# Norm statistics moved from ScalarE and GpSimd to VectorE, with every engine's order written anew

## The chip, the cores and the metric

The kernel runs on one core of one Trainium2 chip. The metric is device time in microseconds (us) of one execution. Its engines are TensorE (PE; its weight loads are the row PEld), VectorE (DVE), ScalarE (ACT), GpSimd (POOL) and SyncE (SP), which here only issues DMAs.

## The reference

Two transformer blocks in a row over 64 sequences of 64 rows by 256 features. What is computed, for each sequence:

```
x   = hidden
x  += attention(layernorm(x) @ w_qkv)        @ w_ao      # self, 16 heads of 16
x  += attention(layernorm(x) @ w_q, ctx @ w_kv) @ w_co   # cross, keys and values from ctx
x  += gelu(layernorm(x) @ w1) @ w2                       # mlp0
lat = x
y   = attention(lat @ q_w, concat(ctx, lat) @ kv_w) @ out_w + lat
out = gelu(rmsnorm(y) @ mlp_w1) @ mlp_w2 + lat           # mlp1
```

Each layernorm subtracts a row's mean and multiplies by one over the root of its variance plus an epsilon; the rmsnorm before the second MLP multiplies by one over the root of the mean square plus an epsilon. All biases, scales and masks are applied. Inputs and output are float32.

## The kernel before, in words

Two sequences make a unit of 128 rows, so there are 32 units, each a chain of the same stages: self attention, cross attention, mlp0, the attention over context and latents ("ctx" and "lat"), mlp1. Products run in float16 in two halves: each operand is written as a high part and a low part, and three matmuls stand for one (`w_hi` with high and low, `w_lo` with high). An activation gets its halves on the row-major side in `pair_*`, and one transposing DMA, issued by SP, brings both to the feature-major side in `turned_*` (or `heads_turned_*` for what attention gives). So a norm runs thus: VectorE adds a projection to the residual (`add_residual`, L1282, or `add_mlp`, L1298); the statistics; ACT applies them (`normalize`, L1920, `xn_*`); GpSimd rounds to the high half (`high_pair`, L2465); VectorE takes the low half (`low_pair`, L1174 and L1177); SP issues the transposing DMA (`across`, L2779); PE uses what it brings.

The statistics before the change are spread over three engines. For the three layernorms (self, cross, mlp0) VectorE runs `bn_stats` (L1165) and `bn_aggr` (L1168), and GpSimd in `root` runs three instructions on 128x1: variance plus epsilon (`var_*`, L2454), the power of minus one half (`rstd_*`, L2456), minus mean times that (`shift_*`, L2459). For the rmsnorm of mlp1 ACT squares and sums the row (`squared_rows`, L1928), and GpSimd runs L2454 and L2456.

No scheduler acts when the kernel is built. For each engine the order of the stages is written out by hand as a list of calls such as `moments(t - 3, "cross")`: a part that fills the pipeline, a loop `for t in range(FILL, SLOTS)` of 24 passes in which every stage of some unit stands once, and a part that drains it. The number taken from `t` is the lag of that stage; the last argument of PE's calls is the PSUM bank. Engines run their lists in order and wait on semaphores, so an instruction that waits holds up all behind it on its engine. SP issues all DMAs from one list too.

VectorE's other work in a pass: `k_spread` and `q_bias_self` (PSUM to SBUF), `masked`, `largest_score`, `shifted` (softmax on 128x512), `denominators` and `divided` (`over_*`, `heads_*`), `heads_low` (L1186), `hidden_lo` (L1288). GpSimd's: `plus_bias`, `added` (mask addend, L2507), `mask_add`, `mask_keys`, `ctx_high`, `ctx_low`, `shifted_ctx` (L2513).

## Time and profile before

| | |
|---|---|
| median of 3 runs | 1072.71 us (1070.87 to 1075.0) |
| profiled execution, its own time | 1074.24 us |
| its span in the trace | 1072.0 us |
| PE busy | 1002.5 us, 94% |
| VectorE busy | 949.5 us, 89% |
| ACT busy | 859.3 us, 80% |
| GpSimd busy | 671.7 us, 63% |
| mean granted TensorE clock | 0.978 |

Busy shares are averages over three stretches: the filling of the pipeline up to about 206 us, the loop up to about 937 us, and the drain. Within the loop every pass takes the same time and shows the same picture, so it is read per pass; the two ends have other limits. A span begins and ends with the first and last record of the trace; the execution's own time is 2.24 us longer.

### The profile page before, as it was taken

To read this page: it belongs to the slowest core of one execution; us is meant where nothing else is said; L and a number is where in the kernel's file an instruction comes from. 1 tells how busy PE (TensorE), PEld (TensorE's weight loads), DVE (VectorE), ACT (ScalarE), POOL (GpSimd) and SP (SyncE) were. 2 spreads that over 40 slices of the span, in tenths; PEclk is the share of its full clock that TensorE was granted. 3 is DMA by queue.
4 is the path that set the end of the run, shared out by engine and by line. 5 is a ranking of instruction groups with operands and counts; after the bars stand their busy time and mean duration, and the time that the engine had idled before them with its cause. 6 is when DMAs were issued, how large, how long until landed. Compare 5 with 4: busy or idle time off the path is not lost.

```text
span 1072.0 us, 46440 instructions
## 1 busy us (share of the span) xinstructions
PE 1002.5 (94%) x19180; PEld 892.1 (83%) x19180; DVE 949.5 (89%) x2008; ACT 859.3 (80%) x1967; POOL 671.7 (63%) x1037
## 2 busy tenths in 40 slices
PE   5777989999999999999999999999999999998988
PEld 5666878888888888888888888888888888887877
DVE  4887988999999999999999999999999999987763
ACT  3447689888888888888889888888888888787995
POOL 3787577666667666666666666666666666755320
PEclk9787999999999999999999999999999999999999
DMA  8652221223322222232222222222222222321111
GB/s 297 208 161 78 46 47 37 50 55 59 49 49 47 54 51 52 55 60 54 50 48 53 54 45 58 56 59 49 50 46 55 50 54 44 67 47 37 32 22 41
DMA packets 169699, 67.70 MB, mean 63 GB/s; under 512 B 151184, under 2 KB 167312, under 8 KB 168464
## 3 DMA queue, kind: packets, MB, share of 16 engines
q1 hardware_dynamic: 169488, 64.72, 26.8%
q8 instruction: 152, 2.49, 1.0%
q14 instruction: 59, 0.48, 0.2%
HBM read 26.93 MB, written 4.19 MB: 29 GB/s over the span
## 4 chain that ended last, share of the span: by engine, by line
PE 30%; ACT 23%; DVE 18%; issue 11%; DMA 11%; SPq 5%; POOL 2%; ACTq 0%; POOLq 0%; DVEq 0%
PE psum L457 9%; ACT staging L2007 7%; PE psum L598 7%; ACT hid_mlp L2007 6%; PE psum L630 5%; DMA turned_cross<-pair_cross 4%; PE psum L470 4%; DMA heads_turned_cross<-heads_pair_cross 3%; ACT L1993 3%; DVE mx_lat L1239 3%; PE psum L564 2%; SPq L2779 2%; ACT parts_mlp L2016 2%; ACT probT_self L1993 1%; SPq L2761 1%
## 5 line engine op out<-in xcount | busy, mean ns | idle before, releaser
L2513 POOL TENSOR_TENSOR late<-late,mx_ctx 128x512 f32<-128x512 f32 x64 | 67.7, 1057 | 103.9 <-DVE mx_ctx L1245 103.9
L2507 POOL TENSOR_TENSOR prob_cross<-prob_cross,add_cross 128x512 f32<-128x512 f32 x64 | 91.1, 1441 | 57.5 <-DVE prob_cross L1229 57.4
L2507 POOL TENSOR_TENSOR prob_self<-prob_self,add_self 128x512 f32<-128x512 f32 x64 | 81.9, 1282 | 38.5 <-DVE prob_self L1229 32.3
L2007 ACT ACTIVATE hid_mlp<-psum,folded,undo_in 128x128 f32<-128x128 f32 x256 | 96.2, 458 | 7.8 <-PE psum L457 7.1
L2007 ACT ACTIVATE staging<-psum,cols,undo_in 128x128 f32<-128x128 f32 x256 | 97.8, 484 | 2.8 <-PE psum L457 2.3
L630 PE MATMUL psum<-hi_m,parts_mlp 128*128 128x256 f16 x512 | 95.3, 275 | 0.3 <-DVE parts_mlp L1288 0.3
L630 PE MATMUL psum<-hi_n,staging 128*128 128x256 f16 x512 | 93.9, 273 | 1.4 <-DVE staging L1288 1.4
L457 PE MATMUL psum<-turned_mlp,hi_m 128*128 128x128 f16 x1024 | 92.3, 219 | 3.1 <-DMA turned_mlp<-pair_mlp 1.4
L457 PE MATMUL psum<-turned_mlp,hi_n 128*128 128x128 f16 x1024 | 90.4, 220 | 0.8 <-DMA turned_mlp<-pair_mlp 0.3
L2484 POOL TENSOR_TENSOR xb<-x,rows 128x256 f32<-128x256 f32 x96 | 82.8, 873 | 10.2 <-DVE x L1298 5.7
L457 PE MATMUL psum<-turned_mlp,lo_m 128*128 128x128 f16 x512 | 88.7, 219 | 0.0
L457 PE MATMUL psum<-turned_mlp,lo_n 128*128 128x128 f16 x512 | 88.1, 220 | 0.0
L457 PEld LDWEIGHTS psum<-turned_mlp,hi_m 128*128 128x128 f16 x1024 | 78.3, 98 | 9.4 <-issue 5.5
L1993 ACT ACTIVATE late<-psum 128x512 f32<-128x512 f32 x128 | 71.7, 596 | 12.3 <-PE psum L584 12.2
L457 PEld LDWEIGHTS psum<-turned_mlp,hi_n 128*128 128x128 f16 x1024 | 78.9, 98 | 2.3 <-issue 1.1
L630 PE MATMUL psum<-lo_m,parts_mlp 128*128 128x256 f16 x256 | 70.2, 274 | 0.0
L630 PE MATMUL psum<-lo_n,staging 128*128 128x256 f16 x256 | 69.8, 273 | 0.0
L598 PE MATMUL psum<-val_ctx,late 128*64 128x34 f32 x1024 | 63.7, 228 | 0.7 <-issue 0.5
L598 PE MATMUL psum<-val_lat,late 128*64 128x34 f32 x1024 | 63.0, 226 | 0.0
L1288 DVE SCALAR_TENSOR_TENSOR parts_mlp<-hid_mlp,hidden_up,parts_mlp 128x512 f16<-128x512 f32 x64 | 57.0, 891 | 6.1 <-ACT parts_mlp L2016 5.1
L598 PEld LDWEIGHTS psum<-val_ctx,late 128*64 128x64 f32 x1024 | 53.3, 140 | 6.3 <-issue 5.8
L1985 ACT ACTIVATE val_lat<-psum,undo 64x128 f32<-64x128 f32 x128 | 47.3, 369 | 12.8 <-PE psum L470 11.0
(262 smaller groups left out, 3766.4 us busy)
## 6 DMA issues: line engine op xcount, KB each, us to landing
xin<-in_x SPq DMA_DIRECT2D x32, 128.0 KB, 2.1
late<-in_ctxT SPq DMA_DIRECT2D x4, 1024.0 KB, 6.0
ctxT<-in_ctxT SPq DMA_DIRECT2D x32, 128.0 KB
late<-in_x SPq DMA_DIRECT2D x4, 1024.0 KB, 5.1
out<-xb SPq DMA_DIRECT2D x32, 128.0 KB, 2.0
staging<-in_w_m SPq DMA_DIRECT2D x2, 1024.0 KB, 7.1
staging<-in_w_n SPq DMA_DIRECT2D x2, 1024.0 KB, 5.0
mask<-in_mask_cross SPq DMA_DIRECT2D x32, 32.0 KB
```

The lines of the kernel that those rows point to most:

```text
L457: last = e.matmul(out_ap, wt[name][:, k, c:c + P], xs[:, k, :], start=(n == 0), stop=(n == 3 * KH - 1))
L470: last = e.matmul(ps[:, 0:H], xs[:, k, :], wt[name][:, k, c:c + H], start=(n == 0), stop=(n == 3 * KH - 1))
L598: last = e.matmul(ps[S * a:S * a + S, p * VW:(p + 1) * VW], probT[s][a][:, j, :], val[s][:, a, p, :], start=(n == 0), stop=(n == len(sets) ...
L630: last = e.matmul(ps[:, 0:H], a, wt, start=(g == 0 and n == 0), stop=(g == 1 and n == 11))
L1239: e.tensor_reduce(max_of(t, h).rearrange("p (r n) -> p r n", r=2), src, AX.X, ALU.max).then_inc(sem["max_" + t], 1)
L1288: e.scalar_tensor_tensor(part[t][g][:, 512:1024], hid[t][g][:, :], hidden_up[t], part[t][g][:, 0:512], ALU.mult, ALU.subtract).then_inc(se ...
L1985: last = e.activation(o, i, ACT.Copy, scale=scale)
L1993: e.activation(probT[t][a][:, :, :], src, ACT.Exp).then_inc(sem["probT_" + t], 1)
L2007: last = e.activation(hid[t][g][:, j * P:(j + 1) * P], ps[:, j * P:(j + 1) * P], ACT.Gelu_apprx_tanh, bias=b1[:, 4 * g + j:4 * g + j + 1], ...
L2484: e.tensor_tensor(o[:, :], a[:, :], row, ALU.add).then_inc(sem["plus_bias_" + t], 1)
L2507: e.tensor_tensor(ch, ch, over_heads(a[:, :]), ALU.add).then_inc(sem["added_" + t], 1)
L2513: e.tensor_tensor(ch, ch, over_keys(max_of("ctx", h)), ALU.subtract).then_inc(sem["shifted_ctx"], 1)
```

## The change

Statistics. For all four norms VectorE now computes the moments and the variance plus epsilon. `moments` runs four instructions for each norm: `bn_stats`, `bn_aggr`, and then for a layernorm minus the mean (`minus_mean_*`) and the shrunk variance (`var_*`); for mlp1 the mean square from mean and variance, and the same with epsilon. ACT's `squared_rows` is gone. GpSimd's `root` keeps the power, and for a layernorm the product of minus mean and `rstd`. Core of the diff:

```diff
 # VectorE, moments(u, t)
-                src, steps, n = residual(t, u), sem["moments_" + t], 2 * u
-                q.wait_ge("moments_" + t, n)
+                src, shrink = residual(t, u), 2.0 ** (-2 * XHAT_UP)
+                steps, n = sem["moments_" + t], 4 * u
...
-                    q.wait_ge({"cross": "x_self", "mlp0": "x_cross"}[t], u + 1)
+                    q.wait_ge({"cross": "x_self", "mlp0": "x_cross", "mlp1": "x_lat"}[t], u + 1)
                 e.bn_stats(bn[t][:, :], src[:, :]).then_inc(steps, 1)
                 q.wait_ge("moments_" + t, n + 1)
-                q.wait_ge("rstd_" + t, 3 * u)
                 e.bn_aggr(mv[t][:, :], bn[t][:, :]).then_inc(steps, 1)
+                q.wait_ge("moments_" + t, n + 2)
+                if t == "mlp1":
+                    e.scalar_tensor_tensor(mean_square[:, :], mv[t][:, 0:1], mv[t][:, 0:1], mv[t][:, 1:2],
+                                           ALU.mult, ALU.add).then_inc(steps, 1)
+                    q.wait_ge("moments_" + t, n + 3)
+                    e.tensor_scalar(var[t][:, :], mean_square[:, :], L1_EPS, shrink, ALU.add, ALU.mult).then_inc(steps, 1)
+                else:
+                    q.wait_ge("rstd_" + t, 2 * u)
+                    e.tensor_scalar(minus_mean[t][:, :], mv[t][:, 0:1], -1.0, None, ALU.mult).then_inc(steps, 1)
+                    e.tensor_scalar(var[t][:, :], mv[t][:, 1:2], L0_EPS, shrink, ALU.add, ALU.mult).then_inc(steps, 1)
 # ScalarE
-            def squared_rows(u):
-                q.wait_ge("x_lat", u + 1)
-                q.wait_ge("rstd_mlp1", 2 * u)
-                e.activation(squared[:, :], residual("mlp1", u)[:, :], ACT.Square, scale=1 / ROOT_H,
-                             accum_out=mean_square[:, :]).then_inc(sem["mean_square_mlp1"], 1)
 # GpSimd, root(u, t)
-                e.tensor_scalar(var[t][:, :], src, eps, shrink, ALU.add, op1=ALU.mult).then_inc(done, 1)
-                q.wait_ge("rstd_" + t, n + 1)
-                e.tensor_tensor(rstd[t][:, :], var[t][:, :], minus_half[:, :], ALU.pow).then_inc(done, 1)
+                q.wait_ge("moments_" + t, 4 * u + 4)
+                q.wait_ge("x_lo_mlp1" if t == "mlp1" else "xn_" + t, u)
+                e.tensor_tensor(rstd[t][:, :], var[t][:, :], minus_half[:, :], ALU.pow).then_inc(sem["rstd_" + t], 1)
                 if t != "mlp1":
-                    q.wait_ge("rstd_" + t, n + 2)
-                    e.tensor_scalar(shift[t][:, :], mv[t][:, 0:1], rstd[t][:, 0:1], -1.0, ALU.mult, op1=ALU.mult).then_inc(done, 1)
+                    q.wait_ge("rstd_" + t, 2 * u + 1)
+                    e.tensor_tensor(shift[t][:, :], minus_mean[t][:, :], rstd[t][:, :], ALU.mult).then_inc(sem["rstd_" + t], 1)
 # SP's loop, a line or two of the new lists
-                load_rest(t - 2)
                 across(t - 3, "cross")
                 across(t - 4, "mlp0")
+                across(t - 7, "mlp1")
+                load_rest(t - 1)
```

Orders. All five lists are new, in the fill, the loop and the drain, and so are PE's bank numbers. Some lags differ: PE's `qk_self` goes from `t - 1` to `t - 2` and stands first in the pass, `v_cross` from `t - 2` to `t - 3`; on VectorE the second half of the "lat" softmax and the low half of cross attention's heads go to the start of the next pass; `load_rest` is one unit earlier. On VectorE the second half of self attention's subtraction of the maximum and both halves of cross attention's (`shifted`) now stand in a row, after all four maxima. In GpSimd's list `plus_bias` of lat stands between `root` and `high_pair` of cross, and `plus_bias` of mlp0 between `root` and `high_pair` of mlp0; before, each pair was adjacent.

The first place is VectorE in the loop, where the layernorm of cross attention gets its statistics. Before:

```order
L1282 SCALAR_TENSOR_TENSOR x<-psum,undo,xb 128x256
L1165 BN_STATS bn_cross<-x 128x6
L1168 BN_AGGR mv_cross<-bn_cross 128x2
L1177 TENSOR_TENSOR pair_self<-xn_self,pair_self 128x256
L1165 BN_STATS bn_self<-xin 128x6
L1168 BN_AGGR mv_self<-bn_self 128x2
L1282 SCALAR_TENSOR_TENSOR x<-psum,undo,xb 128x256
L1165 BN_STATS bn_mlp<-x 128x6
L1168 BN_AGGR mv_mlp<-bn_mlp 128x2
```

The same place now, beginning with the statistics of mlp1 (`bn_mlp<-xb`):

```order
L1165 BN_STATS bn_mlp<-xb 128x6
L1167 BN_AGGR mv_mlp<-bn_mlp 128x2
L1170 SCALAR_TENSOR_TENSOR mean_square<-mv_mlp 128x1
L1173 TENSOR_SCALAR var_mlp<-mean_square 128x1
L1189 SCALAR_TENSOR_TENSOR q_self<-psum,down_q,folded 128x256
L1213 SCALAR_TENSOR_TENSOR spread_self<-psum,down_of_two_self,bias_of_two_self 128x2x128
L1297 SCALAR_TENSOR_TENSOR staging<-staging,hidden_up 128x512
L1291 SCALAR_TENSOR_TENSOR x<-psum,undo,xb 128x256
L1165 BN_STATS bn_cross<-x 128x6
L1167 BN_AGGR mv_cross<-bn_cross 128x2
L1176 TENSOR_SCALAR minus_mean_cross<-mv_cross 128x1
L1177 TENSOR_SCALAR var_cross<-mv_cross 128x1
```

What was two instructions for a layernorm is four in a row, and mlp1 has four that VectorE did not have.

The second place is VectorE further on in the pass, around the low half of the latents' attention heads (`heads_pair_lat`). Before it stands behind cross attention's softmax (`prob_cross`) and mlp0's low half (`parts_mlp`):

```order
L1239 TENSOR_REDUCE mx_cross<-prob_cross 128x8
L1204 SCALAR_TENSOR_TENSOR spread_lat<-psum,down_of_two_lat,bias_of_two_lat 128x2x128
L1258 TENSOR_TENSOR prob_cross<-prob_cross,mx_cross 128x512
L1288 SCALAR_TENSOR_TENSOR parts_mlp<-hid_mlp,hidden_up,parts_mlp 128x512
L1186 TENSOR_TENSOR heads_pair_lat<-heads_lat,heads_pair_lat 128x256
L1239 TENSOR_REDUCE mx_ctx<-late 128x8
```

Now it stands ahead of the masking of cross attention's scores (`prob_cross<-psum,mask`):

```order
L1267 TENSOR_TENSOR prob_self<-prob_self,mx_self 128x512
L1213 SCALAR_TENSOR_TENSOR spread_lat<-psum,down_of_two_lat,bias_of_two_lat 128x2x128
L1195 TENSOR_TENSOR heads_pair_lat<-heads_lat,heads_pair_lat 128x256
L1186 TENSOR_TENSOR pair_self<-xn_self,pair_self 128x256
L1238 TENSOR_TENSOR prob_cross<-psum,mask 128x512
L1248 TENSOR_REDUCE mx_self<-prob_self 128x8
```

GpSimd's addition to `prob_cross` waits for that masking, so it comes after both low halves now.

The third place is SP's queue around the transposing DMA of cross attention's input (`turned_cross`). Before, the four loads of `load_rest` stand right in front of it:

```order
L2779 DMA_TRANSPOSE turned_self<-pair_self 128x4x128
L2758 DMA ctxT<-in_ctxT 128x256
L2759 DMA mask<-in_mask_cross 128x64
L2761 DMA keys_i<-in_mask_keys 64x64 x2
L2779 DMA_TRANSPOSE turned_cross<-pair_cross 128x4x128
```

Now they come after it and after those of mlp0 and mlp1:

```order
L2780 DMA_TRANSPOSE heads_turned_cross<-heads_pair_cross 128x4x128
L2738 DMA xin<-in_x 128x256
L2771 DMA_TRANSPOSE turned_cross<-pair_cross 128x4x128
L2771 DMA_TRANSPOSE turned_mlp<-pair_mlp 128x4x128 x2
L2750 DMA ctxT<-in_ctxT 128x256
```

Only the load of `xin` is left between the two transposing DMAs there.

## Rows read from the trace of the kernel before

**Rows 1.** The page's first part: busy us, share of the span, instructions.
```profile
PE 1002.5 (94%) x19180; PEld 892.1 (83%) x19180; DVE 949.5 (89%) x2008; ACT 859.3 (80%) x1967; POOL 671.7 (63%) x1037
```

**Rows 2.** Fill, loop, drain: length; PE, PEld, DVE, ACT, POOL busy; PEclk, DMA share, GB/s.
```profile
0.00:206.20 206.20, 170.41 (x2838) 148.75 (x2839) 165.27 (x378) 133.89 (x289) 133.67 (x238) 0.90 0.43 119
206.20:936.60 730.40, 710.54 (x14166) 637.46 (x14163) 692.24 (x1442) 615.76 (x1436) 486.26 (x724) 1.00 0.25 52
936.60:1072.00 135.40, 121.56 (x2184) 105.89 (x2181) 92.02 (x190) 109.66 (x244) 51.76 (x77) 0.97 0.18 35
```

**Rows 3.** Waits from 400 to 704.4 us: who waited for whom; total, times, longest.
```profile
DVE over_self L1264 <- PE psum L598: 3.6, 10, 0.4
PE psum L598 <- ACT probT_self L1993: 3.0, 10, 0.3
PE psum L457 <- DMA turned_cross<-pair_cross: 2.5, 4, 0.9
DVE x L1282 <- PE psum L470: 2.2, 4, 0.7
PE psum L470 <- DMA heads_turned_cross<-heads_pair_cross: 1.9, 4, 0.7
DVE parts_mlp L1288 <- ACT parts_mlp L2016: 1.8, 6, 0.3
DVE prob_cross L1229 <- PE psum L564: 1.4, 4, 0.8
DVE x L1298 <- PE psum L630: 1.1, 5, 0.2
```

**Rows 4.** VectorE's timeline in one pass of the loop, start and duration in us.
```profile
709.51 0.42 DVE L1165 BATCH_NORM_STATS2 bn_self<-xin 128x6 f32<-128x256 f32 x1
709.96 0.18 DVE L1168 BATCH_NORM_AGGREGATE mv_self<-bn_self 128x2 f32<-128x6 f32 x1
710.06 0.47 DVE L1282 SCALAR_TENSOR_TENSOR x<-psum,undo,xb 128x256 f32<-128x256 f32 x1
```

**Rows 5.** VectorE's timeline in the setup: small instructions, the second needing the first.
```profile
12.28 0.16 DVE L1045 TENSOR_SCALAR power<-psum 128x2 int32<-128x2 int32 x1
12.48 0.33 DVE L1099 TENSOR_SCALAR row_up_qkv<-cols,power 128x1 f32<-128x1 f32 x2
```

**Rows 6.** Groups by line on VectorE from 400 to 704.4 us: busy, mean ns | idle before.
```profile
L1288 DVE SCALAR_TENSOR_TENSOR parts_mlp<-hid_mlp,hidden_up,parts_mlp 128x512 f16<-128x512 f32 x20 | 18.3, 913 | 2.2 <-ACT parts_mlp L2016 1.8
L1258 DVE TENSOR_TENSOR prob_self<-prob_self,mx_self 128x512 f32<-128x512 f32 x20 | 17.6, 879 | 0.3
L1258 DVE TENSOR_TENSOR prob_cross<-prob_cross,mx_cross 128x512 f32<-128x512 f32 x20 | 17.3, 864 | 0.3
L1288 DVE SCALAR_TENSOR_TENSOR staging<-staging,hidden_up 128x512 f16<-128x512 f32 x20 | 14.8, 741 | 0.0
L1258 DVE TENSOR_TENSOR late<-psum,mx_ctx 128x512 f32<-128x512 f32 x21 | 14.3, 679 | 0.0
L1186 DVE TENSOR_TENSOR heads_pair_lat<-heads_lat,heads_pair_lat 128x256 f16<-128x256 f32 x10 | 9.5, 948 | 0.0
L1174 DVE SCALAR_TENSOR_TENSOR pair_mlp<-xb,rstd_mlp,pair_mlp 128x256 f16<-128x256 f32 x10 | 7.9, 790 | 0.0
L1191 DVE SCALAR_TENSOR_TENSOR pair_lat<-x,power,pair_lat 128x256 f16<-128x256 f32 x10 | 4.8, 484 | 0.0
L1186 DVE TENSOR_TENSOR heads_pair_self<-heads_self,heads_pair_self 128x256 f16<-128x256 f32 x10 | 4.2, 415 | 0.0
```

**Rows 7.** One piece of the chain of waits in the drain: start, us, what.
```profile
1008.91 0.52 ACT squared L1928 x2
```

**Rows 8.** Timeline around the transposing DMA of cross attention's input.
```profile
712.26 1.12 SPq L2761 DMA_DIRECT2D keys_i<-in_mask_keys  x2
712.41 0.42 DVE L1177 TENSOR_TENSOR pair_cross<-xn_cross,pair_cross 128x256 f16<-128x256 f32 x1
713.50 1.21 SPq L2779 DMA_TRANSPOSE turned_cross<-pair_cross  x1
```

More of the change, by code:

```diff
@@ new lines, in _ @@
+            add_mlp(0, "mlp0")
+            largest_score(2, "cross", 1)
+            shifted(2, "cross", 0)
+            add_residual(3, "self")
+            low_pair(1, "mlp0")
+            lat_low(0)
+            k_spread(5, "self", 1)
+            shifted(2, "cross", 1)
+            denominators(4, "self")
+            divided(4, "self")
+            moments(3, "cross")
+            masked(5, "self", 0)
+            heads_low(4, "self")
+            powers(0, "n2")
+            masked(5, "self", 1)
@@ L1573, in _ @@
                 moments(t - 3, "cross")
[L1574 to L1575 removed]
+                k_spread(t - 2, "self", 1)
                 add_residual(t - 4, "cross")
@@ new lines, in _ @@
+            heads_low(UNITS - 4, "cross")
+            k_spread(UNITS - 3, "cross", 0)
+            hidden_lo(UNITS - 8, "mlp1", 0)
+            largest_both(UNITS - 6, 1)
+            add_residual(UNITS - 7, "lat")
+            shifted(UNITS - 6, "lat", 1)
+            k_spread(UNITS - 3, "cross", 1)
+            moments(UNITS - 7, "mlp1")
+            add_residual(UNITS - 3, "self")
+            moments(UNITS - 3, "cross")
+            add_residual(UNITS - 4, "cross")
+            moments(UNITS - 4, "mlp0")
@@ L2637, in _ @@
-            shifted_ctx(2, 1)
+            ctx_high(4)
+            ctx_low(4)
+            shifted_ctx(1, 0)
+            shifted_ctx(1, 1)
+            mask_keys(3)
+            mask_add(4)
+            root(3, "mlp0")
+            high_pair(3, "mlp0")
+            high_pair(6, "self")
+            plus_bias(3, "mlp0")
+            root(0, "mlp1")
+            added(4, "cross", 0)
+            added(4, "cross", 1)
+            low_mlp(0, "n2")
+            plus_bias(5, "self")
+            plus_bias(1, "lat")
```

1834 lines of the change are left out of this document (891 added, 943 removed).

## The prediction, written before the changed kernel ran

> **What bounds the kernel now.** I read the page's busy shares first. PE leads with 94%, VectorE follows with 89%, ACT has 80%, GpSimd 63% [rows 1]. An average over a filling and draining pipeline says little, so I next cut the span into fill, loop and drain [rows 2]. In the loop the picture is tighter: of 730.4 us PE is busy 710.5 (97.3%), VectorE 692.2 (94.8%), ACT 615.8 (84.3%), GpSimd 486.3 (66.6%), with the TensorE clock fully granted. In the stretch from 400 to 704.4 us a line that a pass runs twice on VectorE stands 20 times [rows 6], so ten passes take 304.4 us: 30.44 us a pass, and the loop's 24 passes fill the middle stretch. Per pass PE works 29.6 us and VectorE 28.84. The loop is thus held by two engines at once: PE has 0.8 us to spare, VectorE 1.6 us. Fill and drain together have less pressure on VectorE (165 of 206 us, 92 of 135 us), and in the drain ACT is busier than VectorE (110 of 135 us).
>
> Third, the waits of ten passes [rows 3]. PE waits for transposing DMAs (2.5 and 1.9 us in ten passes, 0.44 us a pass) and for the exponentials of self attention (0.30 us a pass). VectorE's waits for other engines are five pairs that add up to 10.1 us, 1.01 us a pass. The rest of its 1.60 us of idle time, 0.59 us, is its own: short gaps in which one of its instructions waits for the one before it. These gaps stay whatever PE does. So what VectorE needs for a pass is 30.44 - 1.01 = 29.43 us. The reader is to see that an addition of more than 1.01 us to VectorE's pass makes it the engine that sets the pass.
>
> **What the statistics cost VectorE.** Prices are taken from start to start, since neighbours overlap by some 0.08 us. `bn_stats` to the dependent `bn_aggr` is 709.96 - 709.51 = 0.45 us; `bn_aggr` to an independent successor is 710.06 - 709.96 = 0.10 us [rows 4]. A small instruction to one that needs it is 12.48 - 12.28 = 0.20 us. Two independent ones on 128x1 take 0.33 us together, so the second adds 0.13 us to the first's 0.20 [rows 5]. No row shows a successor waiting on `bn_aggr`; its 0.18 us and the gap of 0.03 us that stands between `bn_stats` (end 709.93) and `bn_aggr` make 0.21.
>
> - mlp1, new on VectorE: 0.45 + 0.21 + 0.20 + 0.13 = 0.99 us.
> - Each layernorm: the wait behind `bn_aggr` goes from 0.10 to 0.21, and two small instructions come at 0.13: + 0.37 us, for three norms 1.11 us.
> - Sum: 2.10 us a pass. From below: if each added small instruction cost no more than its 0.13 us slot and the waits hid, 0.45 + 0.10 + 8 x 0.13 = 1.6 us. From above: if each of the eight cost its dependent 0.20 us, 0.45 + 0.21 + 1.6 + 0.33 (three times 0.11) = 2.6 us. I take 2.10, built from the nearest rows.
>
> With all else equal VectorE needs 29.43 + 2.10 = 31.53 us a pass, 1.09 us more than a pass takes now.
>
> **What else changes on VectorE: its collisions with GpSimd.** Some lines with both inputs in SBUF are longer than their twins [rows 6]: `parts_mlp` 913 against 741 ns, `prob_self` 879 and `prob_cross` 864 against 679 for the same operation out of PSUM, `heads_pair_lat` 948 against 415, `pair_mlp` of mlp1 790 against 484. Per pass: 0.34 + 0.40 + 0.37 + 0.53 + 0.31 = 1.95 us. A new order deals these anew. `heads_pair_lat` now stands before the masking of cross attention's scores, for which GpSimd's big addition waits, so GpSimd has little to do then: - 0.5. The first half of self attention's subtraction likewise: - 0.2. Against that, three of the four halves of `shifted` for self and cross now come in a row, just when GpSimd has `keys_mask` and the context's halves to do; I count + 0.3. Net - 0.4 us, so 31.1 us a pass. The bounds are no collisions at all (31.53 - 1.95 = 29.6, and then PE decides) and half as many again (32.5). I stay near the present value, since no row says how a new order falls.
>
> The Trainium skill ("SBUF — State Buffer", Who interferes with whom) says that a VectorE instruction with two SBUF inputs contends with a GpSimd instruction that reads SBUF, and that the loser fully blocks. The trace agrees with the first part, as the twins above show. By that rule `bn_stats`, with one input, is safe.
>
> **What the others gain.** ACT loses `squared_rows`, 0.52 us a unit [rows 7]. In the loop ACT has 4.8 us a pass to spare, so it is worth nothing there. In the drain ACT is the busiest, and seven or so units pass through its norm there: at most - 3.6 us; I take - 2, as other waits lie between. GpSimd loses four small instructions a pass and is at 67%: nothing in the loop. The chain of one norm is no shorter: VectorE does in 0.2 to 0.3 us what GpSimd did.
>
> **What the new orders gain PE.** Before, `pair_cross` is ready at 712.83 and its DMA is issued at 713.50, because SP is still issuing the loads of `load_rest` until 713.38 [rows 8]. Those loads now come later, so the DMA goes out some 0.6 us sooner, and PE has more products between the projection and `q_cross`. That removes most of the 0.44 us a pass that PE waits for DMAs. Alone it would make the pass 30.0 us. But when VectorE needs 31.1 this only turns into other waiting of PE: worth nothing. Its cover is VectorE's length; if that falls away, the 0.44 us count. Bank numbers cost nothing while PE waits anyway.
>
> **Sum.** Loop: 24 x (31.1 - 30.44) = + 15.8 us. Fill: VectorE has 41 us of idle time there, so the 2.1 us of each of its units mostly fit in; I take + 1. Drain: - 2. Together + 15 us. The profiled execution is 1074.24 us, 2.24 beside its span of 1072.0, so it would be 1089; the median of the runs shown is 1.5 us below it, 1072.7, and by that the new median is 1087.7. Forecast: 1088 us.
>
> **Rivals.**
>
> A, faster: PE stays the bound. If the new order has so few collisions that VectorE needs under 30.0 us (1.5 of the 1.95 us gone), the transposing DMAs' 0.44 us come through: 24 x -0.44 = - 10.6, with the drain - 2: 1060 us. For it: an order that spreads the work may do this, and the list of VectorE puts several colliding lines where GpSimd waits. Against it: GpSimd is busy two thirds of the time, and VectorE would have to be busy over 98% of a pass. It decides from a need of 30.4 downward. Chance 0.22.
>
> B, no change: collisions fall by about 1 us, the need is 30.4 and the pass stays: 1070 to 1076, say 1073. Chance 0.15.
>
> C, much slower: VectorE stalls in its own list. In GpSimd's new list `plus_bias` of lat and of mlp0 stand between the roots and the casts of cross and mlp0, and `low_pair` follows closely on VectorE, with all its later work behind it. A GpSimd instruction takes 486.3 / 724 = 0.67 us in the mean [rows 2]; if the casts of both come later by that and half of it reaches VectorE, it stalls 0.7 us and needs 31.8 us a pass: 24 x 1.36 = 33, with the ends 32, 1105 us. It decides from the point at which a cast ends after VectorE's list has come to the low half. Against it: the addition may pass while ACT applies the norm. Chance 0.11.
>
> The same section of the Trainium skill says that a `tensor_scalar` can enter a two-port mode and then contend with GpSimd too. As a mechanism here: seven of the new small instructions would each wait for a GpSimd instruction under way; with GpSimd busy two thirds of the time and half of the mean 0.67 us still to go, 0.22 us each, 1.6 us a pass, 24 x 1.6 = 38 us on top of the forecast, 1126 us. The setup's small instructions show none of it [rows 5]. Chance 0.02.
>
> The forecast itself (31.1, from 30.6 to 31.6) has 0.50.
>
> **How the numbers follow.** A difference of 0.5%, 5.4 us, is about what a measurement of this kernel can tell from none. Slower by more than that: the forecast but for its lower edge (0.48), C (0.11) and the two-port mechanism (0.02): 0.61. Within: B but for its lower edge (0.13) and the edge of the forecast (0.02): 0.15. Faster: A (0.22) and B's edge (0.02): 0.24. The range leaves out about half of A below, a third of C and the two-port mechanism above: 1062 to 1108; the forecast's own is 1076 to 1100.
>
> **What the profile after would show.** If right: in the loop VectorE is busy over 97% and its waits for PE and ACT are nearly gone, while PE's share falls to about 95.5% and PE waits for VectorE (its `k_spread`, `hidden_lo`, `shifted`) rather than for DMAs; VectorE's busy sum is near 1000 us; the small instructions of `moments` stand 0.13 and 0.20 us apart; `heads_pair_lat` falls to about 0.45 us. Wrong if VectorE stays under 96% busy with a pass of 30.4 us or less (A or B), or if a pass is over 31.6 us; if the change stands in fill or drain, my split is wrong even with the right total.

## The result, and the profile after

The changed kernel takes 1077.34 us (median of 17 runs, 1074.03 to 1079.99), the kernel before 1072.71 us in the same comparison (17 runs, 1069.88 to 1078.22): a ratio of 1.0034, 95% interval 1.0018 to 1.0050. It is slower, as forecast, but by 0.3%, not by the forecast 1.4%. The profiled execution took 1074.87 us, its span is 1073.0 us.

The page's first part and the clock row of its second answer to [rows 1]. The digits of PEclk are tenths of the granted clock in 40 equal slices.

```profile
PE 995.5 (93%) x19180; PEld 887.4 (83%) x19180; DVE 976.1 (91%) x2328; ACT 845.7 (79%) x1903; POOL 629.5 (59%) x909
...
PEclk9898999999999999999999999999999999999999
```

VectorE's busy sum rose by 26.6 us, where "near 1000" had been said. The kernel before has `PEclk9787999` at the head of the same row. The next two windows are the changed kernel's fill and loop, and answer to [rows 2] (length; PE, PEld, DVE, ACT, POOL busy; clock, DMA share, GB/s).

```profile
0.00:200.92 200.92, 163.00 (x2832) 142.72 (x2833) 169.68 (x424) 132.62 (x283) 127.08 (x218) 0.95 0.44 122
200.92:906.33 705.41, 682.37 (x13573) 613.69 (x13571) 676.57 (x1611) 582.60 (x1336) 431.98 (x599) 1.00 0.28 52
```

In the loop PE is busy 96.7% and VectorE 95.9%. Neither is full, though the prediction wanted VectorE over 97%.

A finer cut comes from VectorE's timeline: the starts of its last operation of a unit (`xb<-psum,undo_out,x` of `add_mlp` for mlp1), 32 in each kernel. Before, the first stands at 202.78, the 24th at 902.28 and the last at 1069.40 us. After, they stand at 196.58, 902.35 and 1070.33. So the fill is 6.2 us shorter, 23 passes are 6.3 us longer (a pass 30.69 for 30.41 us in the mean; the median of the 23 is 30.56 for 30.35), and the drain is 0.9 us longer. These two profiled executions differ in span by 1.0 us, the medians by 4.6: the profiled one of after (below, "after" is the changed kernel) is at the quick end of its 17 runs.

Waits from 400 to 704.4 us, VectorE's (the two largest) and PE's, answer to [rows 3]: who waited for whom, total us, times, longest.

```profile
DVE parts_mlp L1297 <- ACT parts_mlp L2026: 5.5, 10, 0.7
DVE pair_mlp L1186 <- POOL pair_mlp L2457: 1.4, 7, 0.2
...
PE psum L584 <- DVE prob_cross L1267: 5.5, 10, 0.8
PE psum L564 <- DVE spread_ctx L1213: 3.0, 10, 0.3
PE psum L470 <- DMA heads_turned_cross<-heads_pair_cross: 0.3, 1, 0.3
```

PE no longer waits for DMAs (0.03 us a pass, 0.44 before) but for VectorE (0.85 us a pass), as forecast. Yet VectorE itself still waits, ten times in ten passes, for ACT's `parts_mlp`. That is the sign of the miss: if VectorE's sum set the pass, it would wait for nobody.

The statistics in VectorE's timeline (start, duration) answer to [rows 4].

```profile
612.95 0.41 DVE L1165 BATCH_NORM_STATS2 bn_mlp<-xb 128x6 f32<-128x256 f32 x1
613.39 0.18 DVE L1167 BATCH_NORM_AGGREGATE mv_mlp<-bn_mlp 128x2 f32<-128x6 f32 x1
613.61 0.22 DVE L1170 SCALAR_TENSOR_TENSOR mean_square<-mv_mlp 128x1 f32<-128x1 f32 x1
613.87 0.15 DVE L1173 TENSOR_SCALAR var_mlp<-mean_square 128x1 f32<-128x1 f32 x1
613.94 0.47 DVE L1189 SCALAR_TENSOR_TENSOR q_self<-psum,down_q,folded 128x256 f32<-128x256 f32 x1
...
615.94 0.43 DVE L1165 BATCH_NORM_STATS2 bn_cross<-x 128x6 f32<-128x256 f32 x1
616.40 0.18 DVE L1167 BATCH_NORM_AGGREGATE mv_cross<-bn_cross 128x2 f32<-128x6 f32 x1
616.62 0.16 DVE L1176 TENSOR_SCALAR minus_mean_cross<-mv_cross 128x1 f32<-128x1 f32 x1
616.69 0.14 DVE L1177 TENSOR_SCALAR var_cross<-mv_cross 128x1 f32<-128x1 f32 x1
616.75 0.48 DVE L1213 SCALAR_TENSOR_TENSOR spread_self<-psum,down_of_two_self,bias_of_two_self 128x256 f32<-128x256 f32 x1
```

mlp1 costs 613.94 - 612.95 = 0.99 us, to the hundredth what was forecast, but partly by luck: a small instruction that needs the one before it starts 0.26 us after it (613.61 to 613.87), not 0.20, and the instruction behind the last follows after 0.07 us, not 0.13, and the two errors cancel. A layernorm costs 616.75 - 615.94 = 0.81, against 0.55 before: + 0.26, forecast + 0.37. Two independent small instructions start 0.07 us apart, not 0.13. The sum is 0.99 + 3 x 0.26 = 1.8 us a pass, for 2.10.

The colliding lines answer to [rows 6] (busy, mean ns | idle before).

```profile
L1267 DVE TENSOR_TENSOR prob_cross<-prob_cross,mx_cross 128x512 f32<-128x512 f32 x20 | 20.3, 1052 | 0.0
L1267 DVE TENSOR_TENSOR prob_self<-prob_self,mx_self 128x512 f32<-128x512 f32 x20 | 15.8, 790 | 0.3
L1297 DVE SCALAR_TENSOR_TENSOR parts_mlp<-hid_mlp,hidden_up,parts_mlp 128x512 f16<-128x512 f32 x20 | 15.5, 775 | 5.5 <-ACT parts_mlp L2026 5.5
L1186 DVE TENSOR_TENSOR pair_mlp<-xn_mlp,pair_mlp 128x256 f16<-128x256 f32 x10 | 5.8, 583 | 1.7 <-POOL pair_mlp L2457 1.4
L1183 DVE SCALAR_TENSOR_TENSOR pair_mlp<-xb,rstd_mlp,pair_mlp 128x256 f16<-128x256 f32 x10 | 4.7, 470 | 0.0
L1195 DVE TENSOR_TENSOR heads_pair_lat<-heads_lat,heads_pair_lat 128x256 f16<-128x256 f32 x10 | 4.1, 413 | 0.0
```

`heads_pair_lat` fell from 948 to 413 ns, `pair_mlp` of mlp1 from 790 to 470, `parts_mlp` and `prob_self` by 138 and 89 twice a pass; `prob_cross` rose from 864 to 1052, twice a pass, and is now the worst. Over all 23 passes, durations beyond those of the undisturbed twins fall from about 2.1 to about 1.2 us a pass: - 0.94, forecast - 0.4. Taking a pass less VectorE's waits for other engines (30.41 - 1.10 = 29.3 before, 30.69 - 0.78 = 29.9 after; "need" below), VectorE needs 29.9 us. The forecast was 31.1. The two measured prices would make 29.3 + 1.8 - 0.94 = 30.2, so some 0.3 us of the fall is not placed.

So what sets 30.56 us? The chain of waits from 600 to 632 us (start, us, what; the last piece is the first, one pass later):

```profile
600.38 0.73 ACT parts_mlp L2026
...
601.13 0.75 DVE parts_mlp L1297
...
603.22 1.96 DVE prob_cross L1267 x2
...
607.15 0.79 DVE spread_ctx L1213 x2
...
608.08 0.70 PE psum L564 x32
...
624.42 0.68 PE psum L457 x12
...
625.96 1.28 ACT L2017
...
629.42 1.50 ACT hid_mlp L2017 x4
...
630.93 0.73 ACT parts_mlp L2026
```

A ring, that is a chain of waits which comes back to its own first piece one pass later: ACT's hidden layer, seven microseconds of VectorE, 17 us of PE without a gap, ACT with a table load (L2017, 1.28 us), and back, 30.55 us later. The chain goes this way in all 23 passes. From the start of one engine's piece to the start of the next one's, the medians are 6.95 us for VectorE, 17.04 for PE and 6.56 for ACT, 30.55 together. VectorE's statistics of mlp1 and of the norms (612.95 to 618.5) lie beside PE's part of the ring. `prob_cross` lies in it, with its collision: 2 x 0.37 us.

### The profile page after: what moved, and what is told of

The parts are those of the page before. It is cut to its first block, busy times and chain, and to the rows that moved or that the text cites. A ratio compares the mean times of both kernels' runs of the same rounds, so it can differ in the third digit from the quotient of the medians.

```text
span 1073.0 us, 46470 instructions
## 1 busy us (share of the span) xinstructions
PE 995.5 (93%) x19180; PEld 887.4 (83%) x19180; DVE 976.1 (91%) x2328; ACT 845.7 (79%) x1903; POOL 629.5 (59%) x909
## 4 chain that ended last, share of the span: by engine, by line
PE 43%; DVE 26%; ACT 19%; issue 9%; POOL 1%; DMA 1%; SPq 1%; ACTq 0%; POOLq 0%; DVEq 0%
PE psum L470 11%; PE psum L457 9%; PE psum L598 7%; PE psum L630 7%; ACT hid_mlp L2017 7%; DVE prob_cross L1267 5%; PE psum L564 5%; ACT L2017 3%; DVE mx_ctx L1248 3%; PE psum L584 3%; DVE parts_mlp L1297 2%; ACT parts_mlp L2026 2%; DVE spread_ctx L1213 2%; DVE mx_cross L1248 2%; ACT staging L2017 1%
## 5 line engine op out<-in xcount | busy, mean ns | idle before, releaser
L2499 POOL TENSOR_TENSOR prob_self<-prob_self,add_self 128x512 f32<-128x512 f32 x64 | 86.9, 1374 | 67.2 <-DVE prob_self L1238 64.3
L2017 ACT ACTIVATE hid_mlp<-psum,folded,undo_in 128x128 f32<-128x128 f32 x256 | 95.5, 455 | 3.5 <-PE psum L457 3.0
L2017 ACT ACTIVATE staging<-psum,cols,undo_in 128x128 f32<-128x128 f32 x256 | 92.9, 460 | 2.7 <-PE psum L457 2.0
L630 PE MATMUL psum<-hi_m,parts_mlp 128*128 128x256 f16 x512 | 90.0, 273 | 0.8 <-DVE parts_mlp L1297 0.8
L2476 POOL TENSOR_TENSOR xb<-x,rows 128x256 f32<-128x256 f32 x96 | 72.2, 752 | 8.5 <-DVE x L1307 4.6
L2003 ACT ACTIVATE late<-psum 128x512 f32<-128x512 f32 x128 | 66.7, 602 | 6.4 <-PE psum L584 5.7
L1297 DVE SCALAR_TENSOR_TENSOR parts_mlp<-hid_mlp,hidden_up,parts_mlp 128x512 f16<-128x512 f32 x64 | 50.1, 783 | 17.1 <-ACT parts_mlp L2026 16.9
L2448 POOL TENSOR_TENSOR rstd_mlp<-var_mlp,minus_half 128x1 f32<-128x1 f32 x64 | 35.4, 553 | 47.1 <-DVE var_mlp L1173 44.7
L1267 DVE TENSOR_TENSOR prob_cross<-prob_cross,mx_cross 128x512 f32<-128x512 f32 x64 | 62.5, 1010 | 0.0
```

The lines of the kernel that those rows point to most:

```text
L630: last = e.matmul(ps[:, 0:H], a, wt, start=(g == 0 and n == 0), stop=(g == 1 and n == 11))
L1267: e.tensor_tensor(in_tiles(prob[t][h][:, :]), src, top, ALU.subtract).then_inc(sem["shifted_" + t], 1)
L1297: e.scalar_tensor_tensor(part[t][g][:, 512:1024], hid[t][g][:, :], hidden_up[t], part[t][g][:, 0:512], ALU.mult, ALU.subtract).then_inc(se ...
L2003: e.activation(probT[t][a][:, :, :], src, ACT.Exp).then_inc(sem["probT_" + t], 1)
L2017: last = e.activation(hid[t][g][:, j * P:(j + 1) * P], ps[:, j * P:(j + 1) * P], ACT.Gelu_apprx_tanh, bias=b1[:, 4 * g + j:4 * g + j + 1], ...
L2476: e.tensor_tensor(o[:, :], a[:, :], row, ALU.add).then_inc(sem["plus_bias_" + t], 1)
```

## The experiments

Pass is the median of the 23 passes and, behind it, their mean; need as above. Pass and need come from one profiled execution each. Each kernel ran beside the kernel before on the same chip; ratios are to that kernel, with 95% intervals.

| | median us (runs) | ratio | pass | mean | need |
|---|---|---|---|---|---|
| before | 1072.4 to 1074.8 (17 to 25) | 1 | 30.35 | 30.41 | 29.3 |
| after | 1077.34 (17) | 1.0034 [1.0018, 1.0050] | 30.56 | 30.69 | 29.9 |
| e1 new orders, old statistics | 1105.99 (5) | 1.0300 [1.0274, 1.0326] | 31.39 | 31.38 | 28.9 |
| e2 old orders, new statistics | 1098.03 (4) | 1.0233 [1.0206, 1.0259] | 31.21 | 31.39 | 31.2 |
| e3 new orders, mlp1's square on ACT | 1090.67 (5) | 1.0160 [1.0133, 1.0186] | 30.84 | 30.92 | 29.3 |
| e4 GpSimd holds | 1070.02 (12) | 0.9977 [0.9961, 0.9993] | 30.38 | 30.40 | 29.5 |
| e5 as e1, square early | 1099.50 (5) | 1.0256 [1.0231, 1.0282] | 31.20 | 31.19 | 28.9 |
| e6 extra outside the ring | 1079.32 (9) | 1.0055 [1.0036, 1.0074] | 30.64 | 30.79 | 30.1 |
| e7 extra inside the ring | 1084.22 (6) | 1.0111 [1.0087, 1.0134] | 30.88 | 30.95 | 30.2 |
| e8 before, loads later | 1070.20 (12) | 0.9980 [0.9961, 0.9998] | 30.33 | 30.37 | 29.5 |
| e9 hold, old statistics | 1100.48 (5) | 1.0227 [1.0202, 1.0252] | 31.17 | 31.14 | 28.7 |
| e10 hold, addition later | 1075.24 (12) | 1.0008 [0.9992, 1.0024] | 30.60 | 30.61 | 29.8 |
| e11 layernorms' statistics old | 1099.46 (6) | 1.0226 [1.0188, 1.0263] | 31.42 | 31.41 | 29.6 |
| e12 small ones in the norms' chain | 1081.71 (9) | 1.0079 [1.0049, 1.0110] | 30.86 | 30.88 | 30.0 |
| e13 the same elsewhere | 1077.14 (12) | 1.0030 [1.0006, 1.0054] | 30.56 | 30.68 | 29.9 |
| e14 hold, heads later | 1081.35 (11) | 1.0076 [1.0051, 1.0102] | 30.87 | 30.91 | 29.9 |

Theory 1 is the prediction's, a sum: VectorE's work sets the pass. Theory 2, a cycle (the ring), came with the profile after.

**e1 and e2, the two halves of the change.** e1 keeps the new orders and banks and takes back the statistics (`moments`, `root` and `squared_rows` as before):

```
                  exponential(t - 6, "lat", 0)
+                 squared_rows(t - 7)
                  exponential(t - 6, "ctx", 0)
...
                  shifted(t - 6, "lat", 1)
-                 moments(t - 7, "mlp1")
```

> The changed kernel's orders, lags and banks with the statistics as before the change: no moments of mlp1 on VectorE, squared_rows back on ACT (five calls ahead of scaled_high in the loop), three small instructions in GpSimd's root, two instead of four in moments. Theory 1 (the statistics are what lengthens the pass; the new orders by themselves help): VectorE's list loses some 1.6 us a pass (0.99 for mlp1, 0.24 for each layernorm, less two small gaps that come back), PE becomes the bound, the pass falls from 30.68 to about 30.0 us, and with the 6 us that the new fill saves the time is about 1058 us, ratio to before 0.986. Theory 2 (the statistics hide in VectorE's idle time; the new order itself made the pass 0.27 us longer through the chain ACT parts_mlp, VectorE shifted, PE): 1074 to 1078 us, ratio 1.002 to 1.005.

e2 is the kernel before with the new `moments` and `root`, `moments(t - 7, "mlp1")` behind `add_residual(t - 7, "lat")` and no `squared_rows`.

> The orders, lags and banks of before with the statistics of the changed kernel: moments of mlp1 right behind add_residual of lat on VectorE, four instructions in each moments, squared_rows gone from ACT, root without the variance. Theory 1: VectorE needs 29.4 us a pass of before plus 1.6 to 1.7, some 31.0, since the collisions with GpSimd stay about 2 us a pass; 24 passes of 0.5 to 0.6 us more, 1085 us, ratio 1.012. Theory 2: the pass stays at 30.4 us, 1071 to 1075 us, ratio 1.000. If my blind sum of 2.1 us for the statistics was right, 1090 us.

In the old orders the sum holds as a mechanism: need and pass are both 31.2 us, and VectorE waits for next to nothing in ten passes. Its size was missed: theory 1 had said 1085 us, and it came to 1098. A part of that is a collision that the edit made worse: `parts_mlp` takes 1215 ns in the mean in e2 and took 913 before, 0.6 us a pass. With the statistics' 1.8 this would be + 2.4 us, and the need grew by 1.9, so 0.5 us is not placed here either.

```profile
DVE parts_mlp L1297 <- ACT parts_mlp L2026: 1.2, 4, 0.3
DVE prob_cross L1238 <- PE psum L564: 0.9, 1, 0.9
```

The prediction's line "with all else equal 31.53" is this kernel. e1 missed by far, and on its own edit: GpSimd waited 22.4 us in ten passes for the square, twice the 11.2 of the kernel before, since it stood late in ACT's list. It was no fair test of the statistics.

**e3 and e5, work taken off VectorE in the new orders.** e3 puts only mlp1's square back on ACT, placed as in e1; e5 is e1 with `squared_rows(t - 7)` at the head of ACT's loop.

> The changed kernel with only the statistics of mlp1 back on ACT (squared_rows) and GpSimd (variance plus epsilon); the layernorms keep their four instructions on VectorE. Theory 1: 0.99 of the 1.6 us leave VectorE, the pass is 30.0 to 30.2 us, 1060 to 1065 us, ratio 0.990. If PE's own length of 29.7 us and its waits set the pass from there, e1 is hardly faster than this one. Theory 2: no change against the changed kernel, ratio 1.003.

> The changed kernel with all of the old statistics, as in e1, but in the loop ACT's squared_rows stands at the head of its list, right after VectorE's lat addition, instead of in front of scaled_high's neighbours: so GpSimd's root of mlp1 should not wait for it as it did in e1. VectorE needs some 28.3 us a pass. Theory of a sum (VectorE's work sets the pass): the loop falls by 24 x 1.6 us, to 1040 to 1060 us. Theory of a cycle (ACT hidden layer -> VectorE mx_cross, prob_cross, spread -> PE -> ACT sets 30.5 to 30.9 us a pass, and the statistics stand outside it): 1070 to 1082 us, VectorE idle for over 2 us a pass, prob_cross still at about 1000 ns. If GpSimd's root of mlp1 is late again (ACT squared among its waits with over 0.5 us a pass), the test is again not fair.

Both are slower, though VectorE needs 0.6 and 1.0 us a pass less. By the mark set for e5, a wait for the square of over 0.5 us a pass, neither is a quite fair test: it is 2.4 us in e3 and 0.59 in e5. But VectorE stood idle 2.3 us a pass in e5 for others, which a sum cannot explain, and e11, e6 and e7 below, which have no square on ACT, say the same. So theory 1 is dead in the new orders.

e3 is explained by the ring. Its chain goes the changed kernel's way in all 23 passes, and the piece that grew is VectorE's, from 6.95 to 7.23 us, as the pair of `prob_cross` now takes 2.29 us for 1.96: GpSimd's work fell differently onto it. For e5's 31.20 the ring as told ("the statistics stand outside it") is not enough. e5 is slower at the ends too: from the start to the first unit's last operation e5 takes 205.4 us and after 196.6, and behind the 24th unit's 174.5 against 170.6. So of e5's 22 us some 12 lie in the loop.

With e2 the change is a square of four: old orders 1072.7 and (new statistics) 1098.0; new orders 1099.5 (old statistics) and 1077.3.

**e4, the collision in the ring.** GpSimd starts its context work only when VectorE is through with `prob_cross`:

```
+ def hold(u): q.wait_ge("shifted_cross", 2 * u + 2)
...
+                 hold(t - 3)
                  mask_keys(t - 3)
```

> The changed kernel with one more wait in GpSimd's loop: before mask_keys it waits until VectorE has done both halves of cross attention's shifted, so that keys_mask, the context's halves and plus_bias of self no longer run beside them. Theory 1 (collisions are part of VectorE's bound): prob_cross falls from 1010 to about 690 ns and the second half of prob_self from 0.84 to 0.69 us, VectorE's pass loses 0.8 to 0.9 us, and the pass goes to 30.0 us, 1062 us, ratio 0.990. GpSimd has 5.1 us of work behind the wait, and about 5.5 us until mx_ctx lets it go on, so the wait itself costs at most 0.3 us a pass. Rival: if not collisions but another limit (PE, the chain through ACT) sets the pass, prob_cross gets shorter and the time stays at ratio 1.003; if the hold delays shifted_ctx, it is slower, 1.006.

```profile
L1267 DVE TENSOR_TENSOR prob_cross<-prob_cross,mx_cross 128x512 f32<-128x512 f32 x20 | 12.9, 684 | 0.0
L1195 DVE TENSOR_TENSOR heads_pair_self<-heads_self,heads_pair_self 128x256 f16<-128x256 f32 x10 | 6.9, 688 | 0.0
```

`prob_cross` fell by 0.37 us twice a pass, the pass by only 0.18 (the mean by 0.29, and the time by 7.3 us): a second ring (ACT `staging`, table load, `probT_self`, VectorE's heads and `late`, PE, ACT), 30.33 us long, takes over in all 23 passes, and GpSimd's displaced work collides with `heads_pair_self` in it. It is the only version of the new orders quicker than the kernel before, by 0.23%.

**e6 and e7, one `bn_stats` outside and inside the ring.** The same 0.42 us instruction at one of two places, the first in e6, the second in e7:

```
+ def extra(u):
+     q.wait_ge("rows_ready", 1)
+     e.bn_stats(spare[:, :], rows[:, 0, :])
...
                  moments(t - 7, "mlp1")
+                 extra(t)
...
                  shifted(t - 3, "cross", 1)
+                 extra(t)
```

> The changed kernel with one more bn_stats of 128x256 a pass on VectorE (its result unused, its input a constant row), placed right behind the statistics of mlp1, outside the cycle. VectorE needs 29.9 + 0.34 to 0.41 = 30.3 us a pass, still below 30.69. Cycle: same time as the changed kernel, 1075 to 1079. Sum: 24 x 0.34 to 0.41 more, 1085 to 1087.

> The same additional bn_stats, now between the two halves of cross attention's shifted and the second half of spread_lat, which the cycle passes through (between parts_mlp and spread_ctx). Cycle: 24 x 0.34 to 0.41 = 8 to 10 us slower than the changed kernel and than e6, 1085 to 1087 (a little less if GpSimd's additions move off prob_cross). Sum: the same as e6, whichever that is.

The median pass grew by 0.08 us outside and by 0.32 inside (the mean by 0.11 and 0.27, the median time by 2.0 and 6.9 us), with a need of 30.1 and 30.2. e6's interval overlaps the changed kernel's, e7's does not. The chain says the same: in e7 the ring's VectorE piece grew from 6.95 to 7.27 us and the others stayed; in e6 the chain passes the additional instruction in none of 23 passes. This is the ring's signature: the place decides, not the engine's sum. Outside it isn't free to the last hundredth: PE's piece is 17.12 us for 17.04, and five of e6's passes are over 31.1 us where after has two. Its profiled execution is also the slowest of its nine.

**e8, the DMAs.** In the kernel before, SyncE's `load_rest(t - 2)` goes behind `across(t - 4, "mlp0")`.

> The kernel before with one edit: in the loop SyncE issues the loads of load_rest behind the transposes of cross and mlp0, not in front of them. The context is used some 15 us later than it lands, so nothing should miss it. If PE's waits for transposes (0.44 us a pass) are worth their size: 24 x 0.3 to 0.44 faster, 1062 to 1066. If they are only turned into other waiting of PE: 1070 to 1074, with the waits for DMAs gone and others, for VectorE or ACT, in their place.

PE's waits for DMAs did not go, they moved (the pair of [rows 3] for `turned_cross` still has 1.6 us in two waits):

```profile
PE psum L470 <- DMA heads_turned_cross<-heads_pair_cross: 2.8, 6, 0.8
PE psum L457 <- DMA turned_mlp<-pair_mlp: 1.9, 5, 0.5
```

The gain is 0.2%, at the edge of what the interval can tell from none, and the price of the 0.44 us stays open.

**e9, e11, e12, e13: what the new statistics give back.** e9 is e4 with e5's statistics; e11 is the changed kernel with only the layernorms' statistics as before; e12 and e13 add two `tensor_scalar` on 128x1, whose result nobody uses, to GpSimd, e13 at the first place and e12 at the second:

```
+ def small(u):
+     for i in range(2):
+         e.tensor_scalar(spare[i][:, :], minus_half[:, :], 1.0, 1.0, ALU.add, op1=ALU.mult)
...
+                 small(t)
                  root(t - 7, "mlp1")
...
+                 small(t)
                  root(t - 4, "mlp0")
```

> e5 (new orders, all of the old statistics, squared_rows early) with the hold of e4 on GpSimd: against e4 it differs in the statistics alone, with the collision on prob_cross gone in both. Sum: VectorE needs 1.6 us a pass less than in e4, so 24 x 1.6 faster than e4, or as far as PE lets it: 1040 to 1060. Cycle: the statistics stand outside, so nothing is won: 1066 to 1076, and up to 1090 if GpSimd's longer list (var, rstd, shift in a row) holds up spread_cross again. Either way e5's pass of 31.20 us should fall by the 0.6 us that its prob_cross lies over two undisturbed ones.

> The changed kernel with the statistics of the three layernorms as before (bn_stats and bn_aggr on VectorE, var, rstd and shift on GpSimd), those of mlp1 all on VectorE as in the change. If the layernorms' chain on GpSimd is what makes the new orders need the new statistics: nearly as slow as e5, pass 31.0 to 31.2, 1088 to 1098, VectorE waiting over 0.4 us a pass for GpSimd's pair_mlp. If it is mlp1's square on ACT: as fast as the changed kernel or faster, 1070 to 1078. By VectorE's sum (6 small instructions fewer, 0.7 us a pass): 1058 to 1062.

> The changed kernel with two more small instructions on GpSimd (tensor_scalar on 128x1, result unused, 0.2 us each) ahead of the root of mlp0, so between cross's and mlp0's norms. If the norms' chain sets or nearly sets the pass: 0.2 to 0.4 us a pass more, 1082 to 1087. If it has slack: 1075 to 1079.

> The same two small instructions, at the head of GpSimd's list, ahead of the root of mlp1, where GpSimd waits 0.94 us for var_mlp. Chain: same time as the changed kernel, 1075 to 1079. GpSimd's sum: as e12.

GpSimd's timeline in after, the norms of cross and mlp0 (start, duration; in brackets the wait before):

```profile
616.92 0.55 POOL L2448 TENSOR_TENSOR rstd_cross<-var_cross,minus_half 128x1 f32<-128x1 f32 x1 [1.95 <-DVE var_cross L1177]
...
618.50 0.40 POOL L2457 CAST pair_cross<-xn_cross 128x256 f16<-128x256 f32 x1
618.86 0.55 POOL L2448 TENSOR_TENSOR rstd_mlp<-var_mlp,minus_half 128x1 f32<-128x1 f32 x1
```

In e11 the same piece is part of the chain of waits (view as above, start and duration), which the fence shows for one pass:

```profile
585.66 0.75 DVE parts_mlp L1297
...
600.95 0.44 DVE bn_cross L1165
...
603.63 0.40 POOL pair_cross L2463
...
604.12 0.46 POOL var_mlp L2453
...
604.65 0.56 POOL rstd_mlp L2455
...
606.33 0.41 POOL pair_mlp L2463
...
607.80 0.83 PE psum L470 x6
...
616.46 0.73 ACT parts_mlp L2026
617.22 0.75 DVE parts_mlp L1297
```

From the cast of cross to `rstd` of mlp0 it is 0.36 us in after and 1.02 in e11: the new `var` is made on VectorE while GpSimd still has cross in hand, the old one waits for its turn on GpSimd. Some 0.26 us of it is a collision: `var_mlp` takes 0.45 us where `var_cross` takes 0.19 (423 to 473 ns in 14 of 23 passes, 191 in the others). Counted from VectorE's `bn_stats` of cross (medians of the 23 passes), VectorE's low half of mlp0 starts 4.98 us later in after, 5.48 in e12, 5.81 in e11, 5.82 in e5 and in e9. In VectorE's list the second `spread_cross` stands behind that low half, and PE's products up to ACT's hidden layer behind it. VectorE's wait for GpSimd there in ten passes is 1.4 us in after, and

```profile
DVE pair_mlp L1186 <- POOL pair_mlp L2463: 7.7, 10, 1.1
```

in e11. This is a third ring, 31.56 us long. It has all of VectorE's list from `parts_mlp` to `bn_cross` in it, the statistics of mlp1 included, then the two norms on GpSimd, and only a short piece of PE and ACT; the pass of e11 is 31.42. The chain takes it in 20 of 23 passes in e11, in 15 in e5, in 18 in e9, in one in e12 and in none in after, e3, e4, e6 and e13. So "the statistics stand outside" was true of the changed kernel's ring alone. (In it `pair_lat` too takes 785 ns for 471 in ten passes, beside GpSimd's context work.) e11 has no square on ACT, so e5's lateness of the square is not needed to explain 31.2 us.

e9 shows it from the other side. Its `prob_cross` is down to 684 ns as in e4, for which its expectation took 0.6 us off e5's 31.20, and the pass stayed at 31.17: in the third ring's reach that collision sets nothing. Both of its theories were far off (1040 to 1060 and 1066 to 1076, 1090 at most, against 1100.48).

e12 gives a direct price: 0.50 us more in the norms' chain makes the pass 0.30 us longer (the mean 0.20), and the same two instructions at the head of the list (e13) make it 0.00 longer. Of the 0.30 the ring's PE piece has 0.18 (17.22 for 17.04 us): PE's six products behind `spread_cross` take 0.83 us for 0.66, as in e11. The other 0.13 is in its VectorE piece, where `parts_mlp` collides more. So the norms' chain just reaches the first ring, with some 0.3 us of slack in after.

**e10 and e14, attempts at a better version.** On top of e4, e10 moves `add_residual(t - 7, "lat")` one place back, behind `shifted(t - 6, "lat", 1)`; e14 moves `heads_low(t - 2, "self")` behind `shifted(t - 5, "lat", 0)`.

> The changed kernel with e4's hold, and on VectorE add_residual of lat one step later, behind the second half of lat's shifted scores, for which PE waited in e4 (late, 1.6 us in ten passes) at the end of e4's next cycle (ACT staging, table load, probT_self, pair_lat, VectorE's heads and mx_lat, late, PE). Cycle: the addition's 0.40 us leaves that chain: pass 30.38 down to 30.0 to 30.2, so 4 to 9 us faster than e4, 1061 to 1066. Sum: nothing changes in VectorE's work, 1070. If the next thing is late at once (the statistics of mlp1 come 0.6 us later, and GpSimd's root with them), 1070 to 1074.

> e4 (the changed kernel with GpSimd's hold) and on VectorE the low half of self attention's heads behind the first half of lat's shifted scores, out of GpSimd's context work, with which it collides in e4 (880 for 410 ns, just in e4's cycle). Cycle: pass down by up to 0.4 us, 1062 to 1067. If the transposing DMA of these heads, which starts 1.5 us later, is then late for PE: 1070 to 1080.

Both missed. In e10 PE waited 3.8 us in ten passes for the moved addition itself (`PE psum L584 <- DVE xb L1291`). The addition's result is urgent for nobody, but it reads PSUM bank 5 (`project(t - 6, "lat", 5)` at the end of PE's loop), and PE's next transposes of `late` go into that bank (`prob_turn(t - 6, "lat", 5)`). In e14 PE waited more for `late` (7.1 us in ten passes) and the DMA of cross's heads came late four times. e4 stays the quickest.

## Why the prediction was right and wrong

**The direction** came out as forecast, the size did not, and the direction owes something to luck. The forecast put + 15.8 us on the loop, since VectorE's need was to pass what a pass takes; the loop's 23 passes grew by 6.3 us for another reason, and the need stayed below the pass. By the prediction's own mark of 0.5% the result is "no difference", to which it gave 0.15. Of the 14 us between the forecast + 15 and the + 1.0 of the profiled pair, 9.5 are the loop's, 7.2 the fill's, and the drain takes 2.9 back.

**The statistics' size** (+ 2.10 us a pass): the mechanism was right; a layernorm cost 0.26, not 0.37, as independent small instructions follow each other at 0.07 us, and mlp1's 0.99 was right by two errors that cancel. Measured 1.8, inside the bounds of 1.6 and 2.6. A smaller part of the miss. So is the base: the five pairs that made 10.1 us of waits left out a sixth (`xb` of L1298 for PE, 0.7 us in ten passes), so the need before was 29.3, not 29.43.

**The step that failed on VectorE** is "Net - 0.4 us, so 31.1 us a pass". The collisions fell by 0.94, the need came to 29.9. The text had named the right lines as gainers (`heads_pair_lat`, `prob_self`) and the right loser (`shifted` of cross), but missed `pair_mlp` of mlp1 and `parts_mlp`, which together gave back 0.6 us.

**A premise failed as well**: that the pass is the longer of two sums, PE's and VectorE's. It holds for e2. In the changed kernel the need of 29.9 is below 30.4, the point that rival A named for PE to decide. Neither decided: rings over ACT, VectorE and PE do, at 30.55 (e6 and e7 show it, e4 moves it). Rival A's 1060 us failed on this. Rival B's "the pass stays" came nearest in mechanism, with its need half a microsecond too high; its 1070 to 1076 us miss the 1077.3 narrowly, the forecast of 1088 misses it by 11. Part of the ring could have been had before the run: the order of VectorE's new list between `parts_mlp` and `spread_ctx` was known, and the durations of [rows 6] would have given its VectorE piece but for the new collision. The kernel before was not a pure sum either. Its chain of waits from 608 to 639 us is a ring of 30.53 us as well, over PE, VectorE, SP's queue with the loads of `load_rest`, a transposing DMA, PE and ACT:

```profile
608.41 1.15 PE psum L598 x32
...
622.62 3.20 DMA turned_cross<-pair_cross
...
638.94 1.15 PE psum L598 x32
```

Its way varies: the chain runs over that DMA in 11 of the 23 passes and over ACT's `probT_self` in all.

**"The chain of one norm is no shorter"** failed, and it matters most. For one norm it is nearly so: from `bn_stats` to `shift` of cross, start to start, it was 1.75 us before and is 1.60. But for two norms in a row on an in-order GpSimd, the second's `var` no longer queues behind the first's cast: in the new orders 0.8 us less up to mlp0's low half. With the old statistics the loop of these orders is 17 us longer (e11 against after, and e9 against e4), the whole kernel 21 to 27 us (ratios 1.0226 against 1.0034, and 1.0227 against 0.9977), with the rest in the fill and the drain. That the queue is what does it is shown by the chain in e11 and, for a smaller delay, by e12; collisions that come with it have a part, and no run takes them out. So the statistics, priced as a pure cost, are a gain in the new orders (22 us, e5 against after, with the square a little late in e5) and a cost in the old ones (26 us, e2 against its own before). The two halves of the change belong together, and priced apart they each look bad.

**Rival C's mechanism** is in the changed kernel, but small: VectorE waits for GpSimd's cast of mlp0 1.4 us in ten passes, 0.14 a pass for the rival's 0.7. In e11 it is 0.77, and the pass is 31.42 us: there the rival's stall has its size. The two-port rival has no sign in its favour: the small `tensor_scalar` took 142 to 156 ns in every pass.

**Transposing DMAs**: right in what was to be seen. The waits went (0.44 to 0.03 us a pass) and turned into waits for VectorE. What covers them is the ring and not, as the prediction had it, VectorE's sum. What they are worth alone e8 did not show.

**The ends**: wrong in sign and size. The fill was + 1, and came out at - 6.2 in the profiled pair, with a granted clock of 0.95 for 0.90 [rows 2]. Both the clock and the change have a part in it. Among kernels with the changed kernel's fill, the first unit is through at 196.3 to 199.4 us with a clock of 0.93 to 0.96 (after, e4, e7, e10, e13, e14) and at 199.0 and 201.0 us with 0.91 to 0.92 (e12, e6). With the old statistics in the layernorms it is 202.4 at 0.94 (e11), and in the old orders the new statistics made it 206.5 for 202.8 (e2). So in the fill too the statistics gain in the new orders and cost in the old ones. How much of the 6.2 us is the clock's stays open. The drain was - 2 and came out at + 0.9. "In the drain ACT is the busiest" was a misreading of [rows 2], where PE has 121.56 us and ACT 109.66. Yet the term for ACT's square had the right sign: the stretch behind the 24th unit is 2.9 us longer in e3, which gives the square back to ACT, than in after, and 0.8 us shorter in e2 than before. The new orders of the drain took more than it gave.

## What to carry to other kernels

A pass whose two busiest engines both have a few per cent to spare was set here by a ring of waits, before the change and after it: write down the chain until its first piece comes back, and price an edit by whether it stands in that ring. Then look for the next ring: three took turns here, each one edit away from the other. Placing the same small instruction inside and outside is a cheap and sharp test (0.32 against 0.08 us for one, 0.30 against 0.00 for the other), and the chain's pieces, summed by engine, say what grew. Moving work to a busier engine can pay when it takes a queueing place out of a chain over an in-order engine; and orders tuned for one division of work are no ground on which to judge the other.
